# A layernorm, complex scan and FP4 feed-forward kernel: both parts of the scan's result turned by TensorE, six pairs scaled by GpSimd

## The reference

```python
xn = layernorm(x)
# 1: a convolution with a complex exponential, as a recurrence over the rows of a sequence
filt = phazor_init * phazor ** t ; conv = causal_conv(filt, xn) + last_conv * phazor ** (t + 1)
attn = real(conv * (1 - |phazor|))
# 2: a feed-forward block; both operands of each product are rounded to FP4 in blocks of 16
q(v) = grid[searchsorted(mid, |v / s|)] * sign(v) * s      # s = max |v| of the block / 6
h    = silu(q(xn) @ q(w_gate).T) * (q(xn) @ q(w_up).T)     # 352 columns
out  = x + attn + q(h) @ q(w_down).T
```

## Time and profile before

| | |
|---|---|
| median of three runs | 120.85 us |
| the profiled execution, its own time | 120.19 us |
| its span in the profile | 118.4 us |
| TensorE, VectorE, ScalarE, GpSimd busy | 109.8, 103.4, 101.9, 100.9 us |

### The profile page before, as it was taken

The page is one execution under the profiler, slowest core; times in us unless marked ns, Lnnn a source line. Parts: engine busy times, 40 slices in busy tenths (PEclk is TensorE's granted clock), DMA queues, the critical chain, the costliest instruction groups (busy, mean ns, idle before and its releaser), DMA issues.

```text
span 118.4 us, 2375 instructions
## 1 busy us (share of the span) xinstructions
PE 109.8 (93%) x671; PEld 84.8 (72%) x671; DVE 103.4 (87%) x221; ACT 101.9 (86%) x226; POOL 100.9 (85%) x121
## 2 busy tenths in 40 slices
PE   0999779979989999999999999999999999999991
PEld 0999546636358686877685886787888787989790
DVE  0599998999999999999999999998999899999500
ACT  5298978989999999999999789989988699579850
POOL 4679998896889999999999999999899999998000
PEclk9999999999999999999999999999999999999999
DMA  3896000000000000020002000200020011020202
GB/s 95 251 295 263 3 0 0 3 6 3 0 0 0 0 0 6 0 89 0 0 0 97 0 3 0 80 9 6 0 89 0 0 41 53 0 89 0 91 28 66
DMA packets 3468, 4.92 MB, mean 42 GB/s; under 512 B 512, under 2 KB 1664, under 8 KB 3456
## 3 DMA queue, kind: packets, MB, share of 16 engines
q1 hardware_dynamic: 3312, 4.77, 12.3%
q10 hardware_dynamic: 144, 0.00, 0.1%
HBM read 2.67 MB, written 2.10 MB: 40 GB/s over the span
## 4 chain that ended last, share of the span: by engine, by line
PE 72%; ACT 9%; DVE 9%; issue 3%; DMA 3%; SPq 1%; DVEq 0%; ACTq 0%
PE ps_o L1313 17%; PE ps_g L1245 15%; PE ps_u L1264 14%; PE ps_h L1283 9%; PE ps_u L1271 7%; DMA x_all<-x_in 3%; PE ps_o L1302 3%; ACT xn L812 3%; PE ps_x L1216 3%; PE ps_x L1230 2%; DVE bn L1532 1%; DVE ps_u L1696 1%; DVE ps_u L1605 1%; ACT silu L856 1%; ACT xbig L833 1%
## 5 line engine op out<-in xcount | busy, mean ns | idle before, releaser
L1245 PE MATMUL ps_g<-wg_T,xq_T 128*128 128x352 f32 x64 | 25.0, 472 | 2.0 <-ACT silu L856 1.2
L1313 PE MATMUL ps_o<-wd_T,hq_T 128*128 128x128 f32 x174 | 23.1, 276 | 0.0
L1313 PEld LDWEIGHTS ps_o<-wd_T,hq_T 128*128 128x128 f32 x174 | 21.6, 192 | 1.8 <-issue 0.4
L1264 PE MATMUL ps_u<-wu_T,xq_T 128*128 128x352 f32 x64 | 22.5, 464 | 0.0
L862 ACT COPY hq_T<-ps_h 128x384 f32<-128x384 f32 x32 | 15.4, 480 | 3.4 <-PE ps_h L1283 3.4
L1283 PE MATMUL ps_h<-ident,hq 128*128 128x128 f32 x96 | 15.9, 275 | 0.3 <-ACT hq_T L862 0.2
L856 ACT ACTIVATE silu<-ps_g 128x352 f32<-128x352 f32 x32 | 14.9, 466 | 1.3 <-PE ps_g L1245 0.9
L1696 DVE TENSOR_TENSOR ps_u<-silu,ps_u 128x704 f32<-128x704 f32 (+1 forms) x17 | 14.3, 843 | 1.7 <-PE ps_u L1264 1.6
L1264 PEld LDWEIGHTS ps_u<-wu_T,xq_T 128*128 128x128 f32 x64 | 11.3, 190 | 5.3 <-DVE hq L1743 1.2
L1735 DVE TENSOR_TENSOR ps_u<-ps_u,inv 128x704 f32<-128x704 f32 (+1 forms) x17 | 14.5, 852 | 0.4
L1743 DVE TENSOR_TENSOR hq<-ps_u,den 128x704 f32<-128x704 f32 (+1 forms) x16 | 13.3, 839 | 1.6 <-PE ps_u L1271 1.4
(11 more groups left out here) (168 smaller groups left out, 247.5 us busy)
## 6 DMA issues: line engine op xcount, KB each, us to landing
x_all<-x_in SPq DMA_DIRECT2D x7, 256.0 KB, 5.4
out<-x_all SPq DMA_DIRECT2D x7, 256.0 KB, 2.0
w_raw<-w_in SPq DMA_DIRECT2D x2, 192.0 KB, 3.7
x_all<-x_in SPq DMA_DIRECT2D x2, 128.0 KB, 2.2
out<-x_all SPq DMA_DIRECT2D x4, 64.0 KB, 1.7
w_raw<-w_in SPq DMA_DIRECT2D x1, 176.0 KB, 4.0
par<-params_in ACTq DMA_DIRECT2D x1, 3.5 KB, 2.5
```

The source lines that it names most:

```text
L1245: pe.matmul(ps_g[:, 0:I], x_cols(t), wg_T[:, :], start=True, stop=True).then_inc(s_gate, 1)
L1264: pe.matmul(slot(q)[:, j, 0:I], x_cols(t), wu_T[:, :], start=True, stop=True).then_inc(s_up, 1)
L1313: m = pe.matmul(out_cols(t), hq_T[t % NHT][:, c * P:(c + 1) * P], wd_T[:, c, :], start=False, stop=(c == NCH - 1), skip_group_check=True)
```

## The change

`YSUM` becomes empty: GpSimd's eight `add_parts` are gone, and TensorE turns both parts of every tile, `y_re` and `y_im`. `BY_POOL` grows from pair 12 to pairs 4, 6, 8, 10, 12 and 13: five more `copy_codes` on ScalarE and `scale_codes` on GpSimd, five `scale_h` fewer on VectorE. `XH` becomes 0: the first half of the first group goes the way of the second, over GpSimd. Group 1 of `x` is loaded by an instruction on ScalarE's queue, behind the parameters, where SP issued it as its third load. Of 32 dummies 17 stay, and the calls of all lists stand in another order. The functions themselves are the same; every line behind the removed load has a number that differs by a few.

```diff
-    XH = 1
-    YSUM = (0, 1, 2, 3, 4, 5, 6, 7)
+    XH = 0
+    YSUM = ()
     WIDE = (1,)
-    BY_POOL = (12,)
+    BY_POOL = (4, 6, 8, 10, 12, 13)
...
-            sp.dma_start(x_all[:, TG:2 * TG, :], x_tiles[1]).then_inc(s_x[1], 16)
...
             act.dma_start(par[:, :], params_in[:, :]).then_inc(s_par, 16)
+            act.dma_start(x_all[:, TG:2 * TG, :], x_tiles[1]).then_inc(s_x[1], 16)
...
-            keep_warm(27, 0)
-            round_first(0)
+            keep_warm(16, 0)
+            in_table(0)
             round_weight(0)
-            keep_warm(1, 0)
             round_weight(1)
...
```

More of the change, by code:

```diff
@@ L1387, in _ @@
             sum_down(4)
+            sum_down(5)
+            turn_xq(4, 1)
             turn_h(7)
-            sum_down(5)
+            gate_tile(15)
+            round_h(5)
             sum_down(6)
-            turn_h(8)
-            round_h(5)
-            gate_tile(15)
-            turn_h(9)
-            turn_xq(4, 1)
+            gate_tile(16)
+            sum_parts(4)
+            sum_parts(5)
             up_tile(14)
             up_tile(15)
-            gate_tile(16)
-            sum_parts(4)
+            gate_tile(17)
@@ L1416, in _ @@
+            sum_down(8)
+            turn_xq(5, 1)
+            turn_h(11)
+            sum_parts(8)
+            round_h(7)
+            sum_down(9)
+            gate_tile(19)
+            up_tile(18)
+            turn_xn(4)
+            sum_down(10)
+            up_tile(19)
+            sum_parts(9)
+            gate_tile(20)
             turn_h(12)
-            sum_parts(8)
-            sum_down(10)
+            sum_parts(10)
+            round_h(8)
+            sum_down(11)
+            sum_parts(11)
@@ L1446, in _ @@
+            sum_down(15)
             up_tile(22)
             up_tile(23)
-            sum_parts(12)
+            turn_h(17)
+            gate_tile(24)
             sum_parts(13)
+            round_h(10)
+            sum_parts(14)
+            turn_h(18)
+            sum_parts(15)
             gate_tile(25)
-            sum_down(15)
-            round_h(10)
-            turn_h(18)
-            gate_tile(26)
-            sum_parts(14)
-            sum_parts(15)
             up_tile(24)
             up_tile(25)
-            turn_h(19)
@@ L1476, in _ @@
             sum_parts(18)
+            turn_xn(6)
+            sum_down(19)
+            turn_h(20)
+            up_tile(26)
+            gate_tile(27)
+            up_tile(27)
             sum_parts(19)
             round_h(12)
-            gate_tile(29)
+            gate_tile(28)
+            turn_h(21)
             turn_xn(7)
             up_tile(28)
+            sum_down(20)
+            turn_h(22)
+            sum_parts(20)
+            gate_tile(29)
+            sum_parts(21)
             up_tile(29)
-            sum_down(20)
@@ L1484, in _ @@
             turn_h(23)
-            gate_tile(30)
-            round_h(13)
             sum_down(21)
-            sum_down(22)
-            sum_down(23)
-            turn_h(24)
-            sum_parts(20)
-            up_tile(30)
-            sum_parts(21)
             sum_parts(22)
             sum_parts(23)
+            sum_down(22)
+            gate_tile(30)
+            turn_h(24)
+            round_h(13)
+            sum_down(23)
             turn_h(25)
+            gate_tile(31)
+            up_tile(30)
@@ L1497, in _ @@
+            sum_parts(24)
             up_tile(31)
-            gate_tile(31)
+            sum_down(24)
             turn_h(26)
-            sum_down(24)
+            sum_parts(25)
+            sum_parts(26)
+            round_h(14)
+            turn_h(27)
             sum_down(25)
-            turn_h(27)
             sum_down(26)
-            round_h(14)
-            sum_parts(24)
-            sum_parts(25)
+            turn_h(28)
             sum_down(27)
-            sum_parts(26)
             sum_parts(27)
-            turn_h(28)
@@ L1883, in _ @@
             stat_shift(1)
+            product(1)
             maxima_h(1)
```

598 lines of the change are left out of this document (286 added, 312 removed).

## The result

The changed kernel takes 122.1 us (median of seven executions, 121.99 to 123.58) against 120.85 us (seven, 120.4 to 121.63): a ratio on record of 1.0137, interval 1.0105 to 1.0168 (the two medians alone give 1.0103). A later session gave 122.32 us against 120.67, 1.0168 (1.0119 to 1.0218). The forecast of 123.7 us had the sign, and its range holds the time, but the forecast cost of 2.85 us over 120.85 is more than twice the 1.25 us measured (1.65 us in the later session).

What follows compares the result with a forecast made beforehand. TensorE's instruction pace was taken to bound the long stretch. Terms 3.4 + 0.3 - 0.5 = +3.2 us gave 123.4 us from the profiled execution, 124.05 from the median; forecast 123.7 us, range 120.6 to 126.2.

Steps and rivals of the forecast that it cites:

- y's transposes in the stretch: Long TensorE-full stretch: 28 added transposes of y at 0.12 us each, +3.4 us, with nothing to hide under.
- GpSimd, VectorE and ScalarE in the stretch: Long stretch: GpSimd 3.2 us less, VectorE 4.2 less, ScalarE 3.7 more work; counted as 0 because TensorE paces it.
- the start: Before the long stretch: -0.5 us taken, between -2.0 and +2.5, from an earlier shift against four more GpSimd calls.
- the tail: After the long stretch: four added transposes of y belong to the last tiles, two between last `turn_h` and `sum_down`; +0.3 us.
- I count 0: Long stretch: VectorE's 4.2 us less work can only give back part of TensorE's 1.9 us of waits; entered as 0.
- the 3 to 4 that were to show the forecast right: Sign of a right forecast: eighth gate product to rounding of the last pair is 3 to 4 us longer.
- rival 1: Long stretch: VectorE's relief removes all 1.9 us of waits and the start keeps 1.5 us; 121.2 us, chance 0.10.
- The dear side: Start: four more GpSimd calls for the first half of `x`, about 2.5 us, delaying what ScalarE and TensorE need.
- The cheap side: Start: VectorE's shift comes up to 1.5 us earlier, and removed TensorE calls help; -2.0 us if all is kept.
- Dummies and the load: both 0: Start: sixteen dummies ending earlier free nothing, and group 1's load on another queue costs nothing; each 0 us.
- rival 4: ScalarE becomes the bound, up to 127.7 us, or the clock halves in the start, some 2 us; chance 0.12.
- Rival 3: Long stretch: VectorE, not TensorE, paces it, so it shrinks by 2.5 us; about 117.4 us, chance 0.09.

Runs made afterwards that it cites:

- after_warm: The changed kernel with four dummies more, two calls around the transposes of the second group of `x`: 122.18 us, ratio 1.0105 against the kernel before.
- load_only: The kernel before with group 1 of x loaded by ScalarE's queue and VectorE's first totals ahead of tile 4's moments: 120.77 us, ratio 1.0003.
- before_again: The kernel before once more, unchanged, for a second trace: 120.59 us, ratio 0.9993.
- y_only: The kernel before with the second transpose of y alone, GpSimd's eight sums taken out and nothing else moved: 123.56 us, ratio 1.0254.
- rest_of_after: The start of the kernel before, then the change's work and orders behind the eighth gate product: 123.70 us, ratio 1.0260 against the kernel before.
- shift_first: The kernel before with VectorE's product of pair 1 moved behind the shift of the second statistics block: 120.84 us, ratio 1.0021.
- late_cut: The changed kernel's start with four dummies and its orders to about 44 us, then the old orders and work: 120.28 us, ratio 0.9958 against the kernel before.
- start_of_after: The changed kernel's start up to the eighth gate product, then the old work and orders: 120.07 us, ratio 0.9960 against the kernel before.

## Why the prediction was right in sign and too high

In the order of its terms, against the trace of before (span 118.41 us) and the change at the full clock (after_warm, 120.11 us):

| term | forecast | measured | from |
|---|---|---|---|
| y's transposes in the stretch | +3.4 | +3.3 | 28 x 0.118 us |
| GpSimd, VectorE and ScalarE in the stretch | 0 | -0.9 | waits 2.17 to 1.29 us |
| the start | -0.5 | -0.9 | eighth gate 33.44 to 32.52 us |
| the tail | +0.3 | +0.2 | 7.91 to 8.11 us |
| span | +3.2 | +1.7 | 118.41 to 120.11 us |

The tail's 0.2 us can't be told from none: with the work of before it is 7.72 us in load_only and 8.30 in before_again.

**The price of a transpose was right.** The chain shows 0.23 to 0.24 us for a tile's two, the stretch runs on TensorE from call to call, and y_only pays it alone. The Trainium skill (page "TensorE: Matmul & The Clock Gate", section "Part 4: PE-mode transpose") gives the duration, about 275 ns, for bf16. The 281 to 283 ns of the lines, in float32, agree. The spacing of 0.118 us again is what counted.

**The step that failed is "I count 0" for the other engines' relief**: "this can only give back part of the 1.9 us of waits", and none of it was put in the sum. 0.9 of 2.17 us went, so the stretch is 2.4 us longer and not the 3 to 4 that were to show the forecast right. Most of it wasn't VectorE's relief: y_only, where VectorE keeps all its work, loses 0.6 already, rest_of_after 0.8. A reading that fits is that the engines that TensorE sometimes waits for get its 3.3 us too; but in y_only GpSimd also has 10.2 us less, and which of the two counts more is open. A further 1.3 us of waits stayed in spite of VectorE's 7.6 us of idle time, so rival 1, which let all of them go, went too far. The 122.1 us measured lies between its 121.2 and the 123.7 of the forecast, and nearer to the rival: I had given the waits no part where about two fifths of them went.

**The start was undersized.** It gave 0.9 us against the first trace of before, 1.4 to 1.5 against the second trace of before and rest_of_after. I had weighed -2.0 against +2.5 and taken a small value. The dear side came in part: the second half of the first group is ready on GpSimd at 17.95 us in place of 16.60, 1.35 us later of the 2.5, and TensorE waits 0.43 us for it. The cheap side came, and not only by the steps that I named. TensorE's start, after the change:

```profile
15.35 0.83 PE L1270 MATMUL ps_u<-wu_T,xq_T 128*128 128x352 f32 x2
16.16 0.83 PE L1251 MATMUL ps_g<-wg_T,xq_T 128*128 128x352 f32 x2
...
18.01 0.44 PE L1236 MATMUL ps_x<-ident,xv 128*128 128x128 f32 x2 [0.43 <-POOL xv L500]
```

and VectorE's, which answers to the earlier trace rows:

```profile
17.81 0.87 DVE L1699 TENSOR_TENSOR ps_u<-silu,ps_u 128x704 f32<-128x704 f32 x1
...
24.83 0.18 DVE L1600 SCALAR_TENSOR_TENSOR shift<-ps_u,rstd 128x24 f32<-128x24 f32 x1
```

The up product of tile 0 now fills the time in which the second gate product waits for the silu, so pair 0's product starts at 17.81 us in place of 18.28, with no wait ahead of it, and the shift follows at 24.83 in place of 25.84. The prediction doesn't speak of the order of those two calls. But the shift no longer sets the time. Before, the chain to the eighth gate product runs over it:

```profile
25.84 0.19 DVE shift L1597
26.05 1.26 ACT xn L812 x3
```

In after_warm, where the shift starts at 24.63 us, just in time for the `normalise` behind it, the chain comes another way:

```profile
17.14 0.63 POOL xv L500
17.82 0.45 PE ps_x L1236 x2
...
22.57 0.59 ACT in_im L761
...
24.18 0.68 ACT big L877
24.85 0.88 ACT xn L812 x2
```

It comes from GpSimd's last call on the first group of `x`, which the prediction had on the dear side, and from 22.57 us to the silu ahead of the eighth gate product it runs over ScalarE's list without a break. So "the stretch begins when ScalarE has worked through what the second block of statistics releases" held before the change and not after it. An earlier shift alone gave nothing (shift_first), and GpSimd's way and ScalarE's order now set the 0.9 us; how much each moved call gave isn't shown.

**"Dummies and the load: both 0"** was wrong as a reason: the load was waited for before (1.18 us, then 1.62 in the second trace, and 0.45 us of that reached the eighth gate product one for one), and in load_only its gain is lost behind the 27 dummies. That fewer dummies would keep it is read from the timelines, not run. As a sum it can't be told from the orders.

**The base.** The forecast lay between 123.4 us, from the profiled execution, and 124.05, from the median. The kernel before varies more than the change does (119.78 to 121.66 us in 29 executions of one session, 121.95 to 122.52 in the ten of the change without the fall), so a single execution of it is a poor base, and this one was quick. From 120.19 the 1.7 us of the spans lead to 121.9, the quickest of the changed kernel (121.95); from the median they would lead to 122.5.

**The rivals.** ScalarE did not become the bound (rival 4): it is busy 10.00 of 10 us from 40 to 50, but the idle time of gate products for the silu in the stretch is 0.2 us in the line L1251 above, 0.5 before. The clock half of that rival came true in 3 of 13 executions at about its 2 us, between 23 and 30 us and not, as I had put it, between the dummies and the first table. Rival 3, VectorE as the pace, is out: 3.9 us less work of VectorE in the stretch of rest_of_after than in that of y_only brings it 0.2 us there. The range's upper end, 126.2 us, isn't the half of rival 4 that it is said to be, which is 125.9; nothing here rests on it.

## What to carry to other kernels

Price an added instruction by the time that the chain moves on, then ask separately what the added time does to the waits that are already in the stretch: part of them fills up by itself. Give every reordering in a start its own line in the sum, above all where an independent call slides into a wait for a single buffer. Price a division of work with lists written for it: the change's orders with the old work took 6.3 us more than the kernel before. Parts that only make sense together (a load off one queue, fewer dummies on another engine) can show nothing when they are tried alone.

## What the runs showed of the hardware beyond that

- Idle gaps of 1.47 and 0.40 us of TensorE in the start, with 1.43 us of work in 3.3, came ahead of a stretch of 3.4 us at half the granted clock in both traces of the changed kernel. With four dummies (eight matmul instructions) around the transposes between them, in after_warm, the gaps were 1.19 us and none, and the clock stayed at 1.00. The idle time doesn't always do it: 21 of 25 executions without these dummies show no fall.
- The same 54 dummies took 7.66 us in one trace of before and 8.04 in load_only, as their spacing went from about 0.2 to 0.11 us at 6.7 and at 7.9 us; the profile gives the granted clock as 1.00 throughout. With 27 dummies on the way of the weights this reaches the start; kernels with fewer had a narrow range (0.34 us in twelve executions of late_cut, 0.36 in eleven of twelve of start_of_after, the other being the one with the clock's fall) against 1.2 to 1.9 us before in the sessions with more than ten executions. That the dummies cause the wide range is an inference: those kernels differ in the load and the rest of the start too, and no run changed the dummies alone.
